# A decoder block on one core: the next keys' row passes placed behind the softmax transposes, and the first batch's rows, queries and latent keys reordered

## What is computed

```python
x = x + rg_lru(layernorm(x))                    # gates, a scan over 100 steps, output projection
x = x + xattn(ctx, layernorm(x))                # the part that the change touches
x = x + moe_ffn(layernorm(x))                   # 8 experts of 512 -> 2048 -> 512, one for each token

# xattn, 8 heads of 128: media = ctx, latents = layernorm(x)
xn = layernorm(media) * gamma + beta            # 722 rows
ln = layernorm(latents) * gamma_l + beta_l      # 100 rows
q  = (ln @ Wq + bq) * 128 ** -0.5
k, v = split(concat([xn, ln]) @ Wkv + bkv)      # 822 keys
out = softmax(q @ k.T) @ v @ Wo + bo
```

## Time and profile before

| what | us |
|---|---|
| median of three executions (1116.9 to 1117.81) | 1117.75 |
| the profiled execution | 1119.51 |
| its span, first to last instruction | 1117.3 |
| PE busy, share of the span | 1056.0, 95% |
| DVE busy | 816.1, 73% |
| ACT busy | 559.3, 50% |
| POOL busy | 125.9, 11% |
| mean granted clock of PE, 1 being full speed | 0.967 |

### The profile page before, as it was taken

The page is one execution under the profiler, slowest core; times in us unless marked ns, Lnnn a source line. Parts: engine busy times, 40 slices in busy tenths (PEclk is TensorE's granted clock), DMA queues, the critical chain, the costliest instruction groups (busy, mean ns, idle before and its releaser), DMA issues.

```text
span 1117.3 us, 18332 instructions
## 1 busy us (share of the span) xinstructions
PE 1056.0 (95%) x6142; PEld 959.7 (86%) x6143; DVE 816.1 (73%) x1409; ACT 559.3 (50%) x1101; POOL 125.9 (11%) x108
## 2 busy tenths in 40 slices
PE   8999968989899999898999999999998999999996
PEld 7979957989899899898998989998976778887775
DVE  6986277877788777787787777676657974857981
ACT  3526443634435345354452544564435855846871
POOL 2521100000000000000000000000011221211341
PEclk9999989989989899898998999999999999999999
DMA  9347964324324333333233414459445982955961
GB/s 273 111 125 179 321 237 164 91 101 142 105 88 117 100 108 98 128 117 100 87 95 140 125 47 148 147 160 371 138 134 190 352 318 98 342 208 207 353 238 30
DMA packets 111955, 185.33 MB, mean 166 GB/s; under 512 B 34332, under 2 KB 53276, under 8 KB 109998
## 3 DMA queue, kind: packets, MB, share of 16 engines
q1 hardware_dynamic: 110158, 180.06, 48.1%
q0 software_dynamic: 1760, 4.79, 1.2%
HBM read 148.70 MB, written 37.10 MB: 166 GB/s over the span
## 4 chain that ended last, share of the span: by engine, by line
PE 70%; DVE 9%; DMA 7%; issue 7%; ACT 3%; POOL 2%; SPq 1%; DVEq 0%; ACTq 0%; POOLq 0%
PE bank L615 20%; PE bank L616 20%; PE bank L617 20%; PE bank L1125 4%; DMA gat<-scr_tokens,idc 2%; DMA stage<-in_W 2%; PE bank L1143 1%; DMA w<-in_WoT 1%; PE bank L1142 1%; PE bank L1112 1%; PE bank L1110 1%; POOL out L974 1%; PE bank L1264 1%; ACT wsh L1432 1%; DMA mrow<-scr_rows 1%
## 5 line engine op out<-in xcount | busy, mean ns | idle before, releaser
L615 PE MATMUL bank<-pt_h,xn_h 128*128 128x256 f32 (+1 forms) x576 | 174.9, 304 | 0.0
L616 PE MATMUL bank<-pt_l,xn_h 128*128 128x256 f32 (+1 forms) x576 | 172.2, 299 | 0.0
L617 PE MATMUL bank<-pt_h,xn_l 128*128 128x256 f32 (+1 forms) x576 | 171.8, 298 | 0.0
L1573 DVE TENSOR_TENSOR wsl<-stage,wsh 128x2048 fp32r<-128x2048 f32 x64 | 145.7, 2289 | 22.1 <-ACT wsh L1432 19.9
L615 PE MATMUL bank<-xt_h,qt_h 128*128 128x410 f32 (+1 forms) x384 | 137.4, 358 | 4.3 <-ACT pr L1388 4.3
L616 PE MATMUL bank<-xt_l,qt_h 128*128 128x410 f32 (+1 forms) x384 | 135.1, 352 | 0.0
L617 PE MATMUL bank<-xt_h,qt_l 128*128 128x410 f32 (+1 forms) x384 | 134.9, 351 | 0.0
L1432 ACT CAST wsh<-stage 128x2048 fp32r<-128x2048 f32 x64 | 122.5, 1917 | 20.8 <-PE bank L617 12.6
L615 PEld LDWEIGHTS bank<-pt_h,xn_h 128*128 128x128 f32 x576 | 116.8, 203 | 1.3
L616 PEld LDWEIGHTS bank<-pt_l,xn_h 128*128 128x128 f32 x576 | 116.8, 203 | 0.0
L617 PEld LDWEIGHTS bank<-pt_h,xn_l 128*128 128x128 f32 x576 | 116.7, 203 | 0.0
(11 more groups left out here) (253 smaller groups left out, 2499.1 us busy)
## 6 DMA issues: line engine op xcount, KB each, us to landing
stage<-in_W SPq DMA_DIRECT2D x64, 1024.0 KB, 6.7
scr_q<-st SPq DMA_DIRECT2D x16, 800.0 KB, 4.1
qf<-scr_q SPq DMA_DIRECT2D x8, 1600.0 KB, 8.1
zr<-scr_z SPq DMA_DIRECT2D x16, 800.0 KB, 5.3
rt<-in_ctxT SPq DMA_DIRECT2D x8, 1444.0 KB, 12.7
scr_z<-zf SPq DMA_DIRECT2D x7, 1600.0 KB, 5.2
raw<-in_ctx SPq DMA_DIRECT2D x8, 768.0 KB, 4.5
mrow<-scr_rows SPq DMA_DIRECT2D x16, 361.0 KB, 4.3
```

The source lines that it names most:

```text
L615: pe.matmul(dest, lh, rh, start=start and k == 0, stop=False)
L616: pe.matmul(dest, lh, rl, start=False, stop=False)
L617: last = pe.matmul(dest, ll, rh, start=False, stop=stop and k == n - 1)
L1573: return dve.tensor_tensor(dst, src, high.bitcast(F32), ALU.subtract)
```

## The change

The hand-written order of the attention batch is another one, with the same events. PE's own order is the same in both. The natural norm is done half (`L+ 0`) right behind `Q+ 0` and half at the end; `B+ 1` comes before `N 4`, and the other quarters of the queries and all four `R+` come later. For batch 0 both halves of the natural norm, the `R` events, the loads and the choice of evicting engine in the second half's k units are moved too.

```diff
-    plan = [..., ("N", 3), ("S", 5), ("N", 4), ("B+", 1), ("Z", (0, 0)), ("PT", 3), ("N", 5), ("S", 6), ("Q+", 0),
-            ("Q+", 1), ("Z", (0, 1)), ("Q+", 2), ("Q+", 3), ("Z", (0, 2)), ("E", 6), ("Z", (0, 3)), ("N", 6),
-            ("Z", (1, 0)), ("PT", 4), ("Z", (1, 1)), ("R+", 0), ("PT", 5), ("Z", (1, 2)), ("R+", 1), ("PT", 6),
-            ("R+", 2), ("T+", 0), ("L+", 0), ("Z", (1, 3)), ("T+", 1), ("Z", (2, 0)), ("R+", 3), ...]
+    plan = [..., ("N", 3), ("S", 5), ("B+", 1), ("Z", (0, 0)), ("N", 4), ("PT", 3), ("S", 6), ("N", 5), ("Q+", 0),
+            ("L+", 0), ("Z", (0, 1)), ("E", 6), ("Z", (0, 2)), ("Z", (0, 3)), ("Z", (1, 0)), ("N", 6), ("PT", 4),
+            ("Q+", 1), ("Q+", 2), ("Z", (1, 1)), ("PT", 5), ("Q+", 3), ("Z", (1, 2)), ("PT", 6), ("R+", 0),
+            ("Z", (1, 3)), ("R+", 1), ("R+", 2), ("T+", 0), ("R+", 3), ("Z", (2, 0)), ("T+", 1), ...]
-    rest = [("L", 0), ("X", 0), ("S", 0), ("X", 1), ("X", 2), ("N", 0), ("L", 1), ("S", 1), ("X", 3), ("X", 4), ("S", 2),
-            ("N", 1), ("X", 5), ("PT", 0), ("X", 6)]
+    rest = [("X", k) for k in range(4)] + [("S", 0), ("X", 4), ("N", 0), ("X", 5), ("S", 1), ("X", 6), ("S", 2),
+                                           ("N", 1), ("PT", 0)]
...
-    early = {(1, 2 * k + 1): [("Q", k)] for k in range(ND)}
-    for k in range(ND):
-        early[1, 2 * k] = [("T", k)]
-    by_act = [what == "q" or dc % 2 == 0 or (half, h) < (0, 3) or half == 0 and dc < 3 for what, half, h, dc in q_units]
+    early = {(1, 0): [("R", 2)], (1, 1): [("Q", 0)], (1, 2): [("R", 3)], (1, 3): [("Q", 1)], (1, 4): [("T", 0)],
+             (1, 5): [("T", 1), ("Q", 2)], (1, 6): [("T", 2)], (1, 7): [("T", 3), ("Q", 3)]}
+    by_act = [what == "q" or dc % 2 == 0 or (half, h) < (0, 3) or (dc < 3 if half == 0 else dc == 1 and h % 2 == 0)
+              for what, half, h, dc in q_units]
...
                         load_latents(0)
+                        sp.wait_ge(s_out_a, 16 * HALF)
+                        load_stats(0, mrow0)
                 if not half:
                     write_residuals(range(HALF, B))
-                    write_latent_keys(1)
-                    sp.wait_ge(s_lnout, 16 * B)
                     sp.wait_ge(s_out_a, 16 * B)
                     sp.wait_ge(s_tpl, B)
                     sp.dma_start(rt0[:, :, 0:MEDIA], a["ctxT"][0].rearrange("(c p) m -> p c m", p=P)).then_inc(s_rt, 16)
-                    load_stats(0, mrow0)
-                    sp.wait_ge(s_ltout, 16 * 4)
+                    sp.wait_ge(s_ltout, 16 * 2)
                     load_latent_keys(0)
...
                     load_queries(0)
+                    write_latent_keys(1)
                     sp.wait_ge(s_cout, 16)
                     sp.wait_ge(s_padq, 1)
                     load_bias_rows(0)
...
                     low_queries(half, h)
-                    if h >= HALF:
-                        run(0, [("R", h - HALF)])
+                    if h in (1, 4):
+                        rows_norm(0, h // 4)
+                    elif h >= HEADS - 2:
+                        run(0, [("R", h - HEADS + 2)])
                 if (what, half, h) == ("q", 1, HEADS - 1):
                     dve.wait_ge(s_qp, u + 1)
-                    dve.wait_ge(s_ltout, 16 * 4)
                     ch.add(dve.memset(cqn[:], 0.0))
-                    for k in range(3):
-                        ch.add(dve.memset(pr[k][:, KEYS:KPAD], 0.0))
                     tally(s_padq)
```

More of the change, by code:

```diff
@@ L453, in bc @@
         return vec.rearrange("(o n) -> o n", o=1).broadcast_to([parts, n])
-    plan = [("S", 3), ("N", 2), ("PT", 1), ("S", 4), ("B+", 0), ("PT", 2), ("N", 3), ("S", 5), ("N", 4), ("B+", 1),
[4 rows of a table removed]
+    plan = [("S", 3), ("N", 2), ("PT", 1), ("S", 4), ("B+", 0), ("PT", 2), ("N", 3), ("S", 5), ("B+", 1), ("Z", (0, 0)),
[4 rows of a table added]
             ("N+", 0), ("X+", 0), ("X+", 1), ("X+", 2), ("X+", 3), ("S+", 1), ("S+", 2), ("N+", 1), ("X+", 4), ("X+",
             5), ("PT+", 0), ("X+", 6)]
-    rest = [("L", 0), ("X", 0), ("S", 0), ("X", 1), ("X", 2), ("N", 0), ("L", 1), ("S", 1), ("X", 3), ("X", 4), ("S", 2),
-            ("N", 1), ("X", 5), ("PT", 0), ("X", 6)]
-    after_rest = [(what[:-1], k) for what, k in plan if what in ("S+", "N+", "PT+", "X+", "L+")]
+    rest = [("X", k) for k in range(4)] + [("S", 0), ("X", 4), ("N", 0), ("X", 5), ("S", 1), ("X", 6), ("S", 2),
+                                           ("N", 1), ("PT", 0)]
+    after_rest = [(what[:-1], k) for what, k in plan if what in ("S+", "N+", "PT+", "X+")]
     assert sorted(rest) == sorted(after_rest)
@@ L1882, in _ @@
             ch.add(dve.memset(xn_h[DUP:P, KC - 1, :].bitcast(F32), 0.0))
+            dve.wait_ge(s_ltout, 16 * 4)
+            for k in range(3):
+                ch.add(dve.memset(pr[k][:, KEYS:KPAD], 0.0))
             tally(s_padp)
```

## The result

The changed kernel takes **1068.1 us** (median of 4 runs, 1065.8 to 1069.5) against 1117.8 for the kernel before (4 runs, 1116.9 to 1118.7): a ratio of 0.9554, 95% interval 0.9531 to 0.9576. That is 49.7 us gained where 53.8 were forecast; the range, 1058 to 1084, holds it. Two later groups timed the same kernel again, each on its own chip: 1070.2 against 1124.0 (0.951, 0.9493 to 0.9527) and 1068.5 against 1118.3 (0.9562, 0.9543 to 0.958). The profiled execution took 1069.5 us, its span is 1067.3.

What follows compares the result with a forecast made beforehand. PE was held by waits, chiefly for a DRAM round trip in each loop turn, and slow clock behind them. 41.5 + 14 - 1 = 54.5 us off the profiled 1119.51 gives 1065.0; median 1.8 lower, forecast 1064, range 1058 to 1084.

Steps and rivals of the forecast that it cites:

- The loop: Seven turns of the attention loop: PE's waits ahead of transpose 6 and the slow clock behind them go, 41.5 us gained.
- slim covers: In the loop, low parts of transposes 4 and 5 done 0.5 us each before PE needs them; at worst 1 us lost per turn.
- The cover ahead of `S 0`: In the loop, DVE's `T 3` ends 1.2 us before PE starts the next `S 0`.
- The rival built on it: PE's wait moves to the next `S 0`: 2 us late gives 1078, from about 2.7 us 1104; chance 15%.
- The last batch: `N 6` behind the fourth `wv_l` delays transpose 4's low parts: +1 us, between 0 and 1.3.
- The first batch: Start through first batch: 20.0 us to be had, less 5 for DVE and 1 for the queue: 14 gained, bounds 10.5 to 15.6.
- signs of being wrong: PE waits ahead of L615 at `S 0` for `xt_l`, loop clock 0.5, ACT waits for q writes; also expected DVE without idle 141 to 162.
- Scores: Stretch from the second `c` copy to `Z (1, 2)` of the first batch: 4.3 us wait and 2.7 slow clock go, 7 us gained.
- Units: Stretch between the two `c` copies (q and k units): 7 us gained, with DVE as the bound and PE losing 5 us.
- The 1 us taken for the queue: First batch: latent keys' 1.6 MB right ahead of the second half's q writes on SP's queue, costing 1 us.
- The third rival: The clock falls among the k units: 27 units take 27 us instead of 20, total 1071; chance 5%.
- the 2.3 of the forecast: First batch: by ring order `mrow` pushes residuals and `rt0` back 2.3 us, gaining 12 instead of 14; left out of the sum.

Runs made afterwards that it cites:

- second repeat: The changed kernel timed once more with nothing altered, in the later of two further groups: 1068.5 us, ratio 0.9562 to the kernel before.
- first repeat: The changed kernel timed once more with nothing altered, in the earlier of two further groups: 1070.2 us, ratio 0.951 to the kernel before.

## Why the prediction was right, and where it was off

**The loop, right.** 40.75 us between the marks where 40.5 were forecast (41.5 less 1 for the last batch). The cause, `R 0` with its round trip ahead of the low parts that free transpose 6's banks, is shown twice: with `R 0` put back alone the waits return, with the new order alone they go. What the forecast did not say is that half of it would have come without moving `R 0` behind transpose 6. Both slim covers held: the waits left ahead of L1125 in the loop are at most 0.2 us each. In one of the two repeats distances of 5.88 to 5.94 show that they can cost a tenth.

**Slow clock as half of the loss, right.** Matmuls that do nothing but run in the wait gave 13 us back.

**The cover ahead of `S 0`**, put at 1.2, is 1.6. The 1.2 rests on a PE that is 6.4 us earlier; the distances of the earlier trace rows, 12.38 and 5.80, give 6.6 and a cover of 1.0. The rival built on it did not come. Its mechanism is real, but the clock falls sooner than it said and costs less. At 2.55 us, below its 2.7, it counts the waits alone, 1064 + 17.9 = 1082; measured are 27.2 us more than the changed kernel, with 1.7 us lost by slow clock behind a wait, not the 2.9 of the kernel before, whose waits were longer and stood at another place. So 1104 from about 2.7 us on looks high, but 2.7 was not run.

**The last batch, right.** From 66.33 to 67.24 us, +0.9 where +1 was forecast. Moving the split behind transpose 4 gives 65.71: 1.5 us had been lost there, of which 0.6 before the change already.

**The first batch, mis-sized:** 14 forecast, 11.2 between the marks, inside its bounds of 10.5 to 15.6. That is luck: the bounds do not follow from what is said of them. `R 0` at 139.8 and no queue effect give 14 + 1.2 + 1 = 16.2, `R 0` as late as before 14 - 1.6 = 12.4, and 11.2 lies below that, with `R 0` as early as 139.19. Two of the signs of being wrong came true too: ACT waits for a q write, 3.54 us, and DVE is not without idle from 141 to 162 but idles some 4.5 us. Two terms are off.

- Scores, 7.0 forecast ("4.3 us, PE at score tile 3" and "2.7 of slow clock"), 5.1 measured. The 4.3 us wait went. But PE now waits 1.23 us ahead of transpose 1 of the first batch, for low parts that DVE starts at 186.76. The slow clock gave back 2.0, not 2.7 (58.14 - 4.3 less 53.04 - 1.23); the 2.7 is half of the 5.4 us of the earlier trace rows, which at their mean clock of 0.53 hold 2.5. The other 0.5 us is not accounted for.
- Units, 7 forecast, 6.1 measured. The size was nearly right, its working only in part. The forecast took the price from the sum of DVE's list, twelve evictions among it ("DVE is the bound of this stage, and PE loses 5 us there"). Four evictions more cost nothing, so that sum does not set the pace. What counts is where `R 1` and `R 2` stand: ahead of the first evictions. In all ten profiles with these `R` events and this share of the evictions, wherever the keys' write and `mrow` stand, PE's first wait is the start of `R 0`, from the first `c` copy, less 16.0 us, to within 0.02: 17.79 gives 1.76, 17.94 gives 1.90, 20.52 gives 4.48. `R 0` starts when `rt0` has landed (in the kernel with `mrow` put back, when `mrow` has). So the first two waits, 2.85 us, come from that landing and from DVE's order; the third, 1.74 us, from the staging tile, whose write took 6.5 us from its request at 146.59 to its landing at 153.10 where it took 3.6 with the keys' write elsewhere. The 1 us taken for the queue was too little.
- The slow clock has no price of its own ahead of that landing. In six profiles, the changed kernel and its second repeat among them, the second `c` copy comes 14.30 to 14.35 us behind it, whether the clock had been low for 3 us or for 7. In the first repeat the clock falls behind the landing, and it is 15.75. The third rival, the clock falling among the k units, had 5% and came true in a small way. The forecast argued from 115 to 120 us that short stops don't bring it about; there PE was busy in all 5.00 of 5 us, so that place said nothing on this one. The Trainium skill, TensorE: Matmul & The Clock Gate, A second HAM failure mode: psum-queue depth-cycling, describes a clock that moves to and fro from frequent micro-idles between groups of matmuls. The rows at 144.29 to 149 agree with it so far as the clock falls, to 0.50, without a long wait; it falls there once and not to and fro.

**The order of the queue.** With `mrow` ahead of them the residuals landed 9.5 us after the last was issued at 123.3, and `rt0` went out at 132.85, against 131.24; with `mrow` put back, SP requests it 1.9 to 2.5 us sooner, about the 2.3 of the forecast. With the keys' write ahead of it `R 0` came 1.8 to 2.6 us later. That is the push that the Trainium skill, DMA: Bandwidth & Descriptors, Queues, rings and completion order, lets one expect, which the forecast had mentioned and left out of the sum: a DMA engine takes one queue's descriptors in the order of the ring. It did not decide: `mrow` has to move its bytes somewhere ahead of `R 0` in any case, and putting it back shortens units and scores by 0.4 to 1.3 us, not by 2.3.

## What to carry to other kernels

Find the load whose round trip stands in a list of work ahead of what frees another engine's banks, and read its whole price from marks of one engine, with the clock behind the wait, not from the wait. In a stretch where the DMA share is 1.0, moving a write that everyone needs only moves the wait: price the stretch by its landings and by what stands ahead of the first evictions, not by the sum of one engine's list. And when a gain at the front is a few microseconds, measure it between marks; the total of a run differs by 2 us for reasons that lie elsewhere.

## What the runs showed of the hardware

- **How little idleness takes the clock down, and that it is not the length alone.** At the same place of the loop waits of 1.28 and 1.29 us left the granted clock at 1.00, waits of 1.41 and 1.43 us brought 1.5 us lost by slow clock on top. Seven waits of 2.55 us, with the same work around them, brought it down six times, and once not. 1.90 and 0.95 us with a matmul group between took it to 0.50 as well; in another profile of the same kernel 1.82 and 0.95 us at that place left it at 1.00.
- **Useless matmuls pay.** 84 matmuls of 512 columns, 2.9 us for twelve, in waits that stayed as they were, made the kernel before 13 us faster.
- **A large write ahead of a small one shows in the small one's landing.** With the 1.6 MB of keys requested just behind the queries' load, the next q write took 6.5 us to land; with the keys earlier or later, 3.6. The queries themselves took 10.2 and 9.6 us in two profiles, against 8.7 and 9.5 with the keys elsewhere.
- **Slow clock can be free.** Ahead of a landing that PE had to wait for anyway, 3 us and 7 us of low clock left the same length from landing to the end of the stage, 14.3 us.
